# Part two of a two-layer network: a recurrence chunk in four VectorE operations instead of six, two square roots taken together, and a new order of the steps

## The reference

```
Sk = S^T k_i
S  = S + beta_i * k_i (v_i - Sk)^T
o_i = S^T q_i
```

## Time and profile before

| what | value |
|---|---|
| median of 3 runs | 1373.09 us (1367.09 to 1374.86) |
| the profiled execution | 1367.92 us |
| its span, first to last instruction | 1366.2 us |
| PE busy | 1170.0 us, 86% |
| DVE busy | 926.2 us, 68% |
| ACT busy | 623.3 us, 46% |
| POOL busy | 453.3 us, 33% |
| mean granted clock of TensorE | 0.944 |

### The profile page before, as it was taken

How to read it: one execution, slowest core, us unless ns; L and a number is a source line. 1 busy time by engine, 2 the same in 40 slices (tenths; PEclk the granted TensorE clock), 3 DMA queues, 4 the chain that set the end, 5 groups by cost and what they waited for, 6 DMA issues and landing times.

```text
span 1366.2 us, 19874 instructions
## 1 busy us (share of the span) xinstructions
PE 1170.0 (86%) x6173; PEld 616.5 (45%) x6173; DVE 926.2 (68%) x2401; ACT 623.3 (46%) x1194; POOL 453.3 (33%) x466
## 2 busy tenths in 40 slices
PE   5989889999899998989896751178999999999997
PEld 2434355453554544635444430134555545455453
DVE  3536536657587677776775577988988988898321
ACT  2071743736737447375373410213464454545642
POOL 3031311212333143232333233236446445544510
PEclk8999999999999999999999885579999999999999
DMA  3212030130321414114213168121020220200000
GB/s 99 82 47 71 1 109 9 48 94 33 109 65 42 131 32 134 47 29 138 55 35 67 25 149 200 48 49 44 14 65 19 47 65 8 57 24 8 24 8 8
DMA packets 85756, 79.91 MB, mean 58 GB/s; under 512 B 42800, under 2 KB 63408, under 8 KB 83632
## 3 DMA queue, kind: packets, MB, share of 16 engines
q1 hardware_dynamic: 85680, 79.01, 21.6%
...
## 4 chain that ended last, share of the span: by engine, by line
PE 50%; DVE 25%; ACT 10%; issue 9%; POOL 4%; DMA 1%; SPq 0%; ACTq 0%; DVEq 0%; POOLq 0%
PE ps L1305 10%; PE ps L954 5%; PE ps L1288 5%; DVE arena L1808 4%; ACT arena L1442 4%; PE ps L991 4%; PE ps L923 4%; ACT arena L1404 3%; PE ps L957 3%; PE ps L964 3%; PE ps L980 2%; DVE arena L2075 2%; PE ps L1058 2%; DVE ps L2070 2%; DVE arena L2073 2%
## 5 line engine op out<-in xcount | busy, mean ns | idle before, releaser
L1808 DVE TENSOR_REDUCE arena<-ps 128x4 f32<-128x512 f32 (+2 forms) x192 | 197.8, 1044 | 89.4 <-PE ps L957 86.3
L1305 PE MATMUL ps<-arena,late 128*128 128x512 f32 x512 | 224.5, 592 | 0.0
L1404 ACT ACTIVATE arena<-ps 128x512 f32<-128x512 f32 (+2 forms) x200 | 109.7, 567 | 232.6 <-PE ps L923 105.4
L1442 ACT ACTIVATE arena<-ps 128x1024 f32<-128x1024 f32 (+3 forms) x256 | 169.9, 711 | 30.6 <-PE ps L980 29.5
L753 POOL TENSOR_SCALAR_AFFINE_SELECT arena<-arena 128x512 f32<-128x512 f32 x128 | 82.9, 650 | 291.9 <-ACT arena L1442 290.4
L964 PE MATMUL ps<-mask_qk,ident_b 128*128 128x512 bf16 x505 | 137.6, 390 | 31.2 <-DVE arena L2087 31.1
L1305 PEld LDWEIGHTS ps<-arena,late 128*128 128x128 f32 x512 | 96.2, 190 | 115.8 <-issue 114.1
L1591 ACT ACTIVATE arena<-ps,f_s 128x512 f32<-128x512 f32 x128 | 85.2, 688 | 102.9 <-PE ps L1305 93.9
L1288 PE MATMUL ps<-arena,late 128*128 128x512 f32 x256 | 116.6, 609 | 7.8 <-ACT arena L1591 7.3
L848 POOL TENSOR_TENSOR arena<-arena 128x512 f32<-128x512 f32 x64 | 81.7, 1276 | 120.8 <-DVE slot_T L2104 76.5
L1404 ACT ACTIVATE arena<-ps,arena 128x128 f32<-128x128 f32 (+1 forms) x128 | 62.3, 528 | 124.5 <-DVE arena L1835 49.3
...
## 6 DMA issues: line engine op xcount, KB each, us to landing
...
```

What stands on the lines that cost most here:

```text
L1305: last = pe.matmul(ps[:, ring2.bank(f"{n}{c}"), :], w[:, k, c * P:(c + 1) * P], src[:, k, :], start=(k == 0), stop=(k == HC - 1))
L1404: return act.activation(dst, src(ps[:, bank, :]), func, **kw)
L1442: act.activation(prob[:, gg % 2, 2 * pr:2 * pr + 2, p_off[jt]:p_off[jt] + w], ps[:, bank:bank + 2, 0:w], ACT.Exp).then_inc(p_taken, 1)
L1808: v.tensor_reduce(heads[:, 2 * pr:2 * pr + 2, gs[0]:gs[-1] + 1], ps[:, at:at + 2, 0:len(gs) * w].rearrange("p q (n w) -> p q n w", w=w), X ...
```

## The change

- **The chunk.** `w_s` gets a ninth column, which holds minus v (`v_neg`), and `k_u` a fifth, which holds the old state (`live`). A sum over nine with `negate=True` gives u = v - w S in one operation, and a sum over five gives the new state. Four operations a chunk, `DVE_SCAN` 64 instead of 96. `w_s`, `k_u` and with them `live` lie in SBUF, twice, a quarter of a tile each; `live_u` stays in PSUM. The first product therefore reads two SBUF tiles, the second one SBUF tile and PSUM.
- **Minus v** is written by ScalarE, one copy of 128x128 with scale -1 for each quarter (`negate_v`), after `keep_history`. The first reduce of a quarter waits for it.
- **Roots.** The root of x4 is taken with that of h in one pass of eight operations over 8 columns (`st_both`, `roots`). x4 keeps `moments_x4` and `centred` of its own; the Fori steps, and those after them with both tiles, use this.
- **VectorE's order.** The four sums come first, with two scan operations behind each, then the add for x4 and its moments; `AT_H` is 28 of 64 and `AT_S` 52. In the step that scans tile 1, `norm_x3` of tile 0 comes at operation 56, in front of the sums and the rest of the scan.
- **TensorE's order.** `project_o` after the first block of layer m and `turn_h` after the third (after the third and fourth in the step of tile 1). `turn_x3` stands inside "y", after two of its four token blocks. Fewer idle matmuls: 20 for 28, 26 for 56, none for 3.
- **ScalarE's order.** The squares of h in front of x4, hT in front of the m tiles.

```diff
-        live = [ps[:, 6 + k, 0:QUARTER * HD * HD].rearrange("p (c v d) -> p c v d", v=HD, d=HD) for k in range(2)]
-        live_u = [ps[:, 6 + k, QUARTER * HD * HD:QUARTER * HD * (HD + CH)].rearrange("p (c v j) -> p c v j", v=HD, j=CH)
-                  for k in range(2)]
+        live_u = [ps[:, 6 + k, 0:QUARTER * HD * CH].rearrange("p (c v j) -> p c v j", v=HD, j=CH) for k in range(2)]
...
+        w_s = [c2.take(QUARTER * HD, CH, HD + 1) for _ in range(2)]
+        k_u = [c2.take(QUARTER * HD, HD, CH + 1) for _ in range(2)]
+        live = [tile[:, :, :, CH].rearrange("p (c v) d -> p c v d", v=HD) for tile in k_u]
+        v_neg = [tile[:, :, :, HD].rearrange("p (c v) j -> p c v j", v=HD) for tile in w_s]
+        st_both = slot_T[:, 256:256 + 64].rearrange("p (k a b) -> p k a b", k=2, a=8)
+        st_h, st4 = st_both[:, 0], st_both[:, 1]
...
-                g.tensor_tensor(hn, h1, st_h[:, 5, :].unsqueeze(2).broadcast_to([P, 4, D]), ALU.mult).then_inc(hn_done, 1)
+                g.tensor_tensor(hn, h1, st_h[:, 3, :].unsqueeze(2).broadcast_to([P, 4, D]), ALU.mult).then_inc(hn_done, 1)
...
-            def last_out(t, turn):
-                by_token("y", turn, hid_n, f_w3, a2_act, CREDIT + A2.emptied("n0", t) - 1).then_inc(a2_ready, 1)
-
-            def step(mlp, last, h, before):
+            def last_out(t, turn, beside):
+                by_token("y", turn, hid_n, f_w3, a2_act, CREDIT + A2.emptied("n0", t) - 1, beside).then_inc(a2_ready, 1)
+
+            def step(mlp, last, h, before, o_at=0, h_at=2):
                 now = {hand: t for hand, t in ((A1, mlp), (A2, last)) if t is not None}
                 turn = (now, before)
                 if last is not None:
                     gates_ab(last, turn)
-                    layer_m(last, turn, 0)
-                    layer_m(last, turn, 1)
+                elif mlp is not None:
+                    pe.wait_ge(om_summed, CREDIT + 5)
+                    idle_matmuls(32, 5)
+                for k in range(HC):
+                    if last is not None:
+                        layer_m(last, turn, k)
+                    if mlp is not None and k == o_at:
+                        project_o(mlp, turn)
+                        if last is None:
+                            idle_matmuls(20, 5)
+                    if mlp is not None and k == h_at:
+                        turn_h(mlp, turn)
                 if mlp is not None:
-                    if last is None:
-                        pe.wait_ge(om_summed, CREDIT + 5)
-                        idle_matmuls(32, 5)
-                    project_o(mlp, turn)
-                    if last is None:
-                        idle_matmuls(28, 5)
-                if last is not None:
-                    layer_m(last, turn, 2)
-                    layer_m(last, turn, 3)
-                if mlp is not None:
-                    turn_h(mlp, turn)
                     gates_gu(mlp, turn)
                 if last is not None:
                     layer_n(last, turn, 0)
@@ -1365,20 +1368,17 @@
                 if last is not None:
                     layer_n(last, turn, 2)
                     layer_n(last, turn, 3)
-                    last_out(last, turn)
-                if mlp is not None:
-                    if last is None:
-                        idle_matmuls(56, 5)
+                    last_out(last, turn, (lambda: turn_x3(mlp, turn, 1 - h)) if mlp is not None else None)
+                elif mlp is not None:
+                    idle_matmuls(26, 5)
                     turn_x3(mlp, turn, 1 - h)
-                    if last is not None:
-                        idle_matmuls(3, ring2.bank("n2"))
                 return now
 
...
+            def negate_v(t, h, q):
+
+                act.wait_ge(sc_loaded[h], CREDIT + (t - h) * 16 + 48)
+                wc = s_wu[h].rearrange("p (c j) w -> p c w j", j=CH)
+                act.activation(v_neg[q % 2], wc[:, q * QUARTER:(q + 1) * QUARTER, HD:2 * HD, :], ACT.Copy, scale=-1.0) \
+                    .then_inc(v_negated, 1)
+
+            def keep_history(t, h, q, more=True):
+
+                act.wait_ge(scan_done, CREDIT + t * DVE_SCAN + 4 * QUARTER * (q + 1))
                 cs = slice(q * QUARTER, (q + 1) * QUARTER)
                 act.activation(state[h][:, cs, :, :], live[q % 2], ACT.Copy)
                 act.activation(u_c[h][:, cs, :, :], live_u[q % 2], ACT.Copy).then_inc(hist_kept, 1)
-
-            def step(scanned, mlp, last, done, h):
+                if q < 2:
+                    negate_v(t, h, q + 2)
+                elif more:
+                    negate_v(t + 1, 1 - h, q - 2)
+
+            def step(scanned, mlp, last, done, h, more=True):
                 if last is not None:
                     for c in range(HC):
                         take_ab(last, c)
                 if scanned is not None:
                     keep_history(scanned, h, 0)
+                if mlp is not None:
+                    square_h(mlp)
                 if done is not None:
                     apply_x4(done)
                 if mlp is not None:
-                    square_h(mlp)
+                    take2(A1, "hT", mlp, hn_T).then_inc(a1_act, 1)
                 if last is not None:
                     for c in range(HC):
                         take_m(last, c)
                 if mlp is not None:
-                    take2(A1, "hT", mlp, hn_T).then_inc(a1_act, 1)
                     take_gu(mlp, last, 0)
                 if scanned is not None:
                     keep_history(scanned, h, 1)
@@ -1662,22 +1674,25 @@
                     for c in range(1, HC):
                         take_gu(mlp, last, c)
                 if scanned is not None:
-                    keep_history(scanned, h, 2)
+                    keep_history(scanned, h, 2, more)
                 if last is not None:
                     take_n(last, 0)
                     take_n(last, 1)
-                if scanned is not None:
-                    keep_history(scanned, h, 3)
+                if scanned is not None and last is not None:
+                    keep_history(scanned, h, 3, more)
                 if last is not None:
                     take_n(last, 2)
                     take_n(last, 3)
                 if mlp is not None:
                     apply_x3(mlp, 1 - h)
-                if mlp is not None:
                     take2(A1, "x3T", mlp, x3_T).then_inc(a1_act, 1)
+                if scanned is not None and last is None:
+                    keep_history(scanned, h, 3, more)
 
...
-                    now, now_u, at = live[c // QUARTER % 2], live_u[c // QUARTER % 2], c % QUARTER
+                    half, at = c // QUARTER % 2, c % QUARTER
                     after = live[(c + 1) // QUARTER % 2]
-                    yield o.mark(v.tensor_tensor(w_s, wc[:, c, :, 0:HD].unsqueeze(1).broadcast_to([P, HD, CH, HD]),
-                                                 now[:, at, :, :].unsqueeze(2).broadcast_to([P, HD, CH, HD]), ALU.mult))
-                    yield o.mark(v.tensor_reduce(now_u[:, at, :, :], w_s, X, ALU.add))
-                    yield o.mark(v.tensor_tensor(now_u[:, at, :, :], wc[:, c, :, HD:2 * HD].rearrange("p j v -> p v j"),
-                                                 now_u[:, at, :, :], ALU.subtract))
-                    yield o.mark(v.tensor_tensor(k_u, now_u[:, at, :, :].unsqueeze(2).broadcast_to([P, HD, HD, CH]),
+                    rows = slice(at * HD, (at + 1) * HD)
+                    now_u = live_u[half][:, at, :, :]
+                    yield o.mark(v.tensor_tensor(w_s[half][:, rows, :, 0:HD],
+                                                 wc[:, c, :, 0:HD].unsqueeze(1).broadcast_to([P, HD, CH, HD]),
+                                                 live[half][:, at, :, :].unsqueeze(2).broadcast_to([P, HD, CH, HD]), ALU.mult))
+                    if at == 0:
+
+                        v.wait_ge(v_negated, CREDIT + t * 4 + c // QUARTER + 1)
+                    yield o.mark(v.tensor_reduce(now_u, w_s[half][:, rows, :, :], X, ALU.add, negate=True))
+                    yield o.mark(v.tensor_tensor(k_u[half][:, rows, :, 0:CH], now_u.unsqueeze(2).broadcast_to([P, HD, HD, CH]),
                                                  kt[:, c, :, :].unsqueeze(1).broadcast_to([P, HD, HD, CH]), ALU.mult))
-                    yield o.mark(v.tensor_reduce(ku_sum, k_u, X, ALU.add))
                     if at == QUARTER - 1:
 
                         v.wait_ge(hist_kept, CREDIT + t * 4 + c // QUARTER)
-                    yield o.mark(v.tensor_tensor(after[:, (c + 1) % QUARTER, :, :], now[:, at, :, :], ku_sum, ALU.add))
+                    yield o.mark(v.tensor_reduce(after[:, (c + 1) % QUARTER, :, :], k_u[half][:, rows, :, :], X, ALU.add))
                 o.end('DVE_SCAN')
 
...
+            def roots(t, which):
+
+                o = Order(v, h_done, DVE_H, t, CREDIT)
+                rsqrt(o, which(3), which(2), which(4))
                 o.end('DVE_H')
 
...
```

(48 more changed lines are left out.)

35 lines of the change are left out of this document (17 added, 18 removed).

## The result

The changed kernel takes **1393.94 us** (median of 4 runs, 1391.9 to 1395.84) for 1373.29 before, a ratio of **1.0167** with a 95% interval of 1.0142 to 1.0193. The prediction was 1372, its range 1355 to 1384: wrong, and on the slow side of every case named in it. The profiled execution has a span of 1394.1 us (before 1366.2) and a granted clock of 0.931 (before 0.944).

The account below looks back on a forecast made before the run. VectorE's 53.7 us loop bounds the kernel, TensorE's 51.9 close behind; changed, a loop through GpSimd gives 54.3. Start -4.9, five periods +3.0, turn +1.3, last tiles 0: -0.6, so 1372 us, range 1355 to 1384.

Parts of the forecast that it names:

- The scan chunk: VectorE's scan: a chunk falls from 2.35 to 1.93 us (bounds 1.83 and 2.1), 6.7 us of VectorE a period.
- the lock: VectorE's first product, reading two SBUF tiles, waits on average 0.64 us for a running GpSimd operation; GpSimd held some 0.3.
- D to the add of h1: From D, the last operation of `norm_x3` on VectorE, to the add of h1: 19.6 us, bounds 17.9 and 21.5.
- hT to the last sum: From hT through GpSimd's gates (end at 13.6 us) and products to VectorE's last sum: 21.1 us.
- The start: Scan 0 to the first full step's D: `gates_ab` of tile 0 comes 13 us earlier, most given back, 4.9 gained.
- The third loop: Stretch through GpSimd's gates and products: VectorE stands 5 us before the first sums, taking most of the 6.7 saved.
- TensorE's loop takes over: Rival: TensorE sets a period of 51.9 us; time 1359, chance 0.28; 1350 with the start's gain kept, 0.12.
- The lock bites harder: Rival: waits beside GpSimd make D to the add of h1 21.5, period 56.2 to 56.7, time 1384; chance 0.22.

Follow-up runs that it names:

- e2: Changed kernel whose first product of a chunk reads a fixed dense block of 64 zeros in SBUF instead of the state: 1373.02 us, ratio 0.9998.
- e10: Changed kernel whose first product reads 64 fixed zeros lying 4 words apart in SBUF instead of the state: 1394.8 us, one run.
- e11: Changed kernel whose first product reads 64 fixed zeros lying 5 words apart in SBUF instead of the state: 1388.77 us, ratio 1.0114.
- e12: Changed kernel whose first product reads 64 fixed zeros lying 2 words apart in SBUF instead of the state: 1375.7 us, one run.
- e1: Changed kernel whose first product reads a fixed block of 64 zeros in PSUM instead of the state: 1368.51 us, ratio 0.9950.
- e13: Changed kernel with AT_H 23 for 28, the add of h1 after 5.75 chunks instead of 7: 1375.94 us, ratio 1.0029 to the kernel before.
- e3: Kernel before with only the four-operation chunk, state in SBUF, all orders and root passes as before: 1383.71 us, ratio 1.0065.
- e14: Changed kernel with first product reading fixed zeros in PSUM and AT_H 23 for 28: 1351.49 us, ratio 0.9845 to the kernel before.
- e7: Changed kernel with hT after the last layer m again, on TensorE and ScalarE: 1401.45 us, ratio 1.0221 to the kernel before.
- e8: Five operations a chunk, state in PSUM, changed kernel's order but hT late on TensorE and ScalarE: 1371.38 us, ratio 1.0013 to the kernel before.
- e6: Changed kernel's orders, but five operations a chunk with the state in PSUM, add of h1 at 28 of 80: 1357.15 us, ratio 0.9900.
- e16: e6 with AT_H 24 of 80 for 28, the add of h1 after 4.8 chunks: 1355.97 us, ratio 0.9865 to the kernel before.

## Why the prediction was wrong

- **The failed step is "The scan chunk".** I took 1.93 us, and said of the strides of 5 and 9 words that there was no row for them. The reduces over nine and over five words were right (0.46 and 0.48 forecast, 0.46 and 0.49 measured), and the products' writes into those rows cost nothing that shows (the second product 422 ns, 425 before). The read of 64 elements at 5 words, used four times over, costs 0.2 us: 2.13, past my upper end of 2.1. "0.42 x 16 = 6.7 us of VectorE a period" was (2.35 - 2.13) x 16 = 3.5, before the lock. Runs e2, e10, e11 and e12 show it, and with a read from PSUM (e1) the chunk is 1.93 us, as forecast. With the stride alone taken out, e2 takes 1373.02 us where I had 1372; that it comes so near is in part luck, for its five periods are 53.7 to 57.4 us and not 54.3.
- **"D to the add of h1", 19.6, was 21.1**, by the same term: 7 x 0.2 = 1.4. In the new order that stretch sets the period, so the size came through undamped. That the rest of the term held was luck. e1, with neither the stride nor a locked product, has 19.4 to 20.8 us there, where my lower bound without sum waits and lock was 17.9. x4's moments, waiting beside the gates, account for some 0.5 to 1.9 us of it in each period; I had them only in a rival. e13 shows that the count there was not a detail: with 23 the changed kernel is 18 us faster. I had counted the 7 chunks, and not said that the count could be had otherwise.
- **"hT to the last sum", 21.1, was 22.5.** I had TensorE stand 2 us before hT and gave the layer m behind it 3.44 us whatever it did. It stood 3.4, and in three of five periods the layer took 4.8 to 5.2 us at a clock of 0.67 to 0.71. The prediction gave low clock no place at all.
- **"The start", -4.9, was +3.4.** Counted from the start of the scan, the first `gates_ab` came 9.3 us earlier and not 13, since the 16 chunks of scan 0 took 0.2 us more each. Then the first period took 65.3 us for 60.3: 1.6 up to hT, with `gates_ab` at 9.21 us for 7.13 and waits of 4.40 and 1.68; 2.5 from hT to D; 0.9 on to `gates_ab`.
- **The lock on the product** was priced about right: forecast 0.64 us at five of sixteen chunks, 0.2 a chunk; e2 shows 0.137 a chunk, and 0.5% of the time. It is not a constant of the product: over 0.63 the mean is 0.13 in the changed kernel, 0.23 in e13 and 0.25 in e3. The Trainium skill's rule on who interferes with whom ("SBUF — State Buffer") is borne out: with one operand in PSUM no product was longer than 423 ns. In the changed kernel it was the smaller half of the price of moving `live`; in e13 and e3 it is larger than the stride's 0.2 in VectorE's time.
- **The third loop** stands in the trace as forecast: what VectorE saves turns into a wait at the first sums, for GpSimd, and GpSimd's gates come late because a layer m stands between hT and `gates_gu`. With the lock taken out of my sum, 19.6 less 1.7 plus 0.6 of other waits, I would have had 53 to 54; three of e1's five periods are 53.0 to 53.4. It is no floor, however: e14, with the add after 5.75 chunks, has 50.7 to 52.2 in the same order. And hT behind the last layer m (e7, e8) did not make the period shorter.
- **The rivals.** "TensorE's loop takes over" is what e14, e6 and e16 show (50.7 to 53.2 for my 51.9, but for one period of 55.3 in e16), but only with the product's operand in PSUM. "The lock bites harder" names the right place (D to the add, 21.5 us) and the wrong cause: the stride did it, with the lower clock behind it, and so the time went 10 us past its 1384.
